# A two-layer perceiver block on one core: attention split by halves of the heads, a running maximum of the context, and new queues

## The chip, the cores and the metric

One core of one Trainium2 chip runs the whole program. The metric is device microseconds (us) from the first to the last instruction of one execution, with what lies around them; the median of three executions of the kernel before is 525.72 us (524.66 to 527.62). "Record" below means one instruction as the profile lists it.

## The reference, cut to what matters

The input has 8 batches of 64 tokens of width 128, and a context of 1601 rows for each batch. The kernel holds the 512 tokens as T = 4 tiles of 128 tokens (two batches each).

1. A stack of 4 layers. Each layer has causal self-attention with 16 heads of 8 elements, cross-attention to the first 32 rows of the context, and a gated feed-forward part of width 512. Before each of the three stands an RMS norm.
2. A message-passing block and a small feed-forward block.
3. Cross-attention to the whole context, with 2 heads of 64 elements.
4. One more self-attention layer with 16 heads (it runs through the same pieces as layer index 4).
5. A mixture of 8 experts, two of them chosen for each token.

```python
qkv = h @ Wqkv[l].T + bqkv[l]
q, k, v = jnp.split(qkv, 3, axis=-1)
q = apply_rope(split_heads(q, H), cos, sin)      # x * cos + rot(x) * sin
k = apply_rope(split_heads(k, H), cos, sin)
o = merge_heads(sdpa(q, k, v, causal_bias)) @ Wo[l].T + bo[l]
```

## The kernel before, in words

The work is cut into **pieces**. A piece is a short function of one engine for one layer or batch `i` and one tile or group `g`. `PIECES` lists them by engine with their counts: (4, 4) for the layers, (5, 4) for the parts that the last self-attention shares, (8, 4) for the context (8 batches, in 4 groups of 4, 4, 4 and 1 chunks of 128 rows). `PLACES` gives each piece its place in the queue of its engine. The engine works through its queue in that order and nothing else: a piece that waits holds back all that stands behind it. `BANKS` and `PLACED` say which of the 8 PSUM banks a piece of TensorE writes, and which piece frees it. Dependencies between engines are semaphore waits (`after`). The tables were made outside of the kernel; there is no planner in the code.

The pieces that matter here, for one tile of one layer, in the order of the data:

- `project` (PE, L804 to L809): four products, for Q, rotated Q, K and rotated K. `values` (L811): the V product.
- `rope` (DVE, L1321): multiplies all 512 columns by the cosines and sines. `rope_sum` (POOL, L1605) adds the two halves of Q and of K, `rope_bias` (POOL, L1610) adds the projection's bias after the rotation, and `k_groups` (POOL, L1615) spreads K over four head positions (128x512).
- `bias` (POOL, L1583 to L1594), once a layer: works the bias through the rotation, four operations.
- `causal`, `scores` (PE, L823, L831), `max` (DVE, L1331) and `shift` (DVE, L1334) over 1024 columns, `exp` (ACT, L1167), `turn` (PE, eight transposes, L839), `turned` (ACT, L1170), `weigh` (PE, L849; it needs `vblk`, DVE, L1326).
- Then `recip`, `o`, `turn_o`, `oT`, `out`, `y1` (DVE, L1353) end the self-attention. The cross-attention (L863 to L903, `y2`) and the gated part (L908 to L920, `y3`) follow.

The first pieces of TensorE's queue are `mem_vp.3` and `mem_vp.1` (L794), products for the cross-attention that need `wm`; the first `turn1` (L803) stands behind them.

For a batch `i` of the context: `c_moments` (DVE, L1452), `c_power` and half of the normalizing (POOL), `c_spread` (ACT, the other half), `c_turn`, `c_keys`, `c_scores` (PE), `c_squares` (ACT), `c_sums` (DVE), `c_rnorm` (POOL, L1674 and L1675), `c_scaled` (DVE, L1463). When all four groups are scaled, `top` (DVE) takes the maximum over the 13 chunks in one reduction (L1469) and over the tile's own scores (L1471). `top_turn`, `top_row`, `top_diag`, `top_spread` make of it one value for a column, `shifted` (DVE, L1483) subtracts it, `weights` (ACT, L1262) takes the exponentials, and `sum_ctx` (PE, L1063) sums.

The context of batch `b` is loaded by the SP queue (L1707) into one of two buffers. From the third batch on it waits until batch `b - 2` has been normalized (POOL) and spread (ACT). The experts' weights are loaded by the same queue before batch 4.

Of the kernel before, what the change touches and what calls it, by code (L numbers as in the profile page):

```python
# [14 lines left out]
P = 128  # L15
# [49 lines left out]
        "turn1": LAYERED5, "project": LAYERED5, "values": LAYERED5, "causal": LAYERED5, "scores": LAYERED5, "turn": LAYERED5,  # L65
        "weigh": LAYERED5, "turn_o": LAYERED5, "out": LAYERED5, "turn2": LAYERED, "qc": LAYERED, "cmask": LAYERED,
# [11 lines left out]
        "square1": LAYERED, "norm1": LAYERED, "hT1": LAYERED5, "exp": LAYERED5, "turned": LAYERED5, "oT": LAYERED5,  # L78
# [9 lines left out]
        "rope": LAYERED5, "vblk": LAYERED5, "max": LAYERED5, "shift": LAYERED5, "recip": LAYERED5, "o": LAYERED5, "y1": LAYERED5,  # L88
# [5 lines left out]
        "qk1_taken": TILED, "l_scaled": TILED, "c_moments": GROUPED, "c_sums": GROUPED, "c_scaled": GROUPED, "top": BATCHED,  # L94
# [6 lines left out]
        "mem_copy": (1, 1), "bias": (LAYERS + 1, 1), "x_zero": (2, 1),  # L101
        "pow1": LAYERED, "rope_sum": LAYERED5, "rope_bias": LAYERED5, "k_groups": LAYERED5, "base": LAYERED, "kc": LAYERED,
# [21 lines left out]
    "x_scaled": "qk1_taken l_scaled c_scaled top top_row top_diag shifted",  # L124
# [11 lines left out]
    "turn1": (1, "hT1"), "project": (1, "rope"), "values": (1, "vblk"), "causal": (4, "shift"), "turn": (2, "turned"),  # L136
    "weigh": (1, "o"), "turn_o": (1, "oT"), "out": (1, "y1"), "turn2": (1, "hT2"), "qc": (1, "qcT"), "cmask": (2, "cshift"),
# [15 lines left out]
HELD = {"scores": "causal", "cscores": "cmask", "up": "gate"}  # L153
# [3 lines left out]
    "mem_kp": (31, 59),  # L157
    "mem_vp": (23, 1, 4, 0, 46, 56, 49, 39),
    "turn1": (3, 2, 10, 9, 93, 85, 105, 111, 170, 161, 194, 209, 251, 238, 293, 277, 533, 515, 595, 620),
    "project": (7, 5, 16, 12, 95, 87, 107, 115, 173, 164, 197, 211, 254, 241, 295, 280, 536, 516, 597, 625),  # L160
    "values": (6, 11, 30, 17, 98, 88, 113, 120, 174, 169, 200, 214, 266, 243, 298, 282, 537, 517, 598, 626),
    "causal": (14, 8, 24, 19, 101, 91, 112, 124, 176, 167, 206, 216, 257, 247, 304, 284, 565, 523, 604, 628),
    "scores": (15, 13, 26, 20, 102, 96, 117, 125, 177, 175, 208, 221, 262, 250, 307, 292, 570, 526, 606, 631),
    "turn": (21, 18, 35, 29, 109, 103, 127, 132, 185, 180, 218, 226, 269, 259, 315, 301, 579, 535, 613, 635),
    "weigh": (28, 22, 40, 34, 114, 106, 130, 137, 187, 184, 222, 229, 272, 264, 319, 306, 587, 554, 617, 637),
    "turn_o": (32, 25, 45, 38, 118, 108, 135, 141, 190, 189, 225, 235, 275, 270, 324, 308, 599, 559, 621, 639),
    "out": (36, 27, 48, 44, 121, 110, 139, 144, 193, 191, 231, 237, 278, 273, 326, 312, 602, 561, 624, 641),
    "turn2": (43, 33, 55, 54, 126, 116, 145, 151, 198, 196, 236, 242, 286, 281, 329, 318),
# [1895 lines left out]
```

How the kernel before makes its waits and increments, by code:

```python
        def step(eng, name, instruction):  # L667
            instruction.then_inc(s[name], 1)
            steps[name] += 1
            eng.wait_ge(s[name], steps[name])
# [1 line left out]
        def after(eng, od, p, i, g=0):  # L673
            if i >= 0 and g >= 0:
                eng.wait_ge(s[SIGNAL.get(p, p)], od.count[p, i, g])
# [1 line left out]
        def after_all(eng, od, p, i):  # L678
            if i >= 0:
                eng.wait_ge(s[SIGNAL.get(p, p)], od.last(p, i))
# [18 lines left out]
        def take(pe, od, p, i, g):  # L699
            for users in od.bank[p, i, g][1]:
                for f, j, k in users:
                    pe.wait_ge(s[SIGNAL.get(f, f)], od.count[f, j, k])
            return held(od, p, i, g)
# [39 lines left out]
        def open_pool(pool):  # L744
            pool.wait_ge(s["par_set"], 1)
            pool.wait_ge(s["y_moments"], 1)
            nc.gpsimd.tensor_tensor(lg[:], mv[:, :, 1], par[:, 0:1].to_broadcast([P, T]), ALU.add).then_inc(s["y_power0"], 1)
            pool.wait_ge(s["y_power0"], 1)
            nc.gpsimd.tensor_tensor(rstd[:], lg[:], par[:, 1:2].to_broadcast([P, T]), ALU.pow).then_inc(s["y_power"], 1)
# [1 line left out]
        def open_dve(dve):  # L751
# [4 lines left out]
            nc.vector.memset(vblk[:], 0.0).then_inc(s["vector_step"], 1)  # L756
            steps["vector_step"] += 1
            dve.wait_ge(s["x_loaded"], 16)
            for t in range(T):
                last = nc.vector.bn_stats(st[:, t, :], x[:, t, :])
            last.then_inc(s["y_stats"], 1)
            dve.wait_ge(s["y_stats"], 1)
            for t in range(T):
```

## Time and profile before

| what | us |
|---|---|
| three executions: median, range | 525.72, 524.66 to 527.62 |
| the execution that was profiled | 524.75 |
| its span, first to last instruction | 522.5 |
| PE, DVE, ACT, POOL busy | 460.1, 361.8, 251.1, 252.9 |
| granted TensorE clock, mean | 0.97 of full |

The profiled execution is 2.25 us longer than its span and 0.97 us shorter than the median. A busy PE is not PE at its peak: records of small products overlap and their ends are modelled. The profile's page gives the busy time by engine, the chain of work that ended last, and groups of instructions by line; the trace behind it can be read in stretches. Stages overlap in this kernel: the layers run from some 15 to 253 us, the messages from 213 to 317, the context from 262 to 450, the last self-attention from 375 to 483, and the experts from 451 to the end.

### The profile page before, as it was taken

To read this page: it belongs to the slowest core of one execution; us is meant where nothing else is said; L and a number is where in the kernel's file an instruction comes from. 1 tells how busy PE (TensorE), PEld (TensorE's weight loads), DVE (VectorE), ACT (ScalarE), POOL (GpSimd) and SP (SyncE) were. 2 spreads that over 40 slices of the span, in tenths; PEclk is the share of its full clock that TensorE was granted. 3 is DMA by queue.
4 is the path that set the end of the run, shared out by engine and by line. 5 is a ranking of instruction groups with operands and counts; after the bars stand their busy time and mean duration, and the time that the engine had idled before them with its cause. 6 is when DMAs were issued, how large, how long until landed. Compare 5 with 4: busy or idle time off the path is not lost.

```text
span 522.5 us, 13720 instructions
## 1 busy us (share of the span) xinstructions
PE 460.1 (88%) x5309; PEld 394.9 (76%) x5318; DVE 361.8 (69%) x944; ACT 251.1 (48%) x592; POOL 252.9 (48%) x370
## 2 busy tenths in 40 slices
PE   2899889897989888999999898986877997999997
PEld 0676776776767767889899887874767886889897
DVE  4868877566656656665687787867686888764644
ACT  2275746754655656545544554423435645413221
POOL 4756786353545334203539994607879852230000
PEclk9999999999989999999999999976897999999999
DMA  8801102000201000000420005500120000000000
GB/s 228 357 3 56 56 1 63 28 10 11 62 3 37 2 1 2 3 3 3 140 68 3 2 3 216 235 1 15 50 65 1 1 1 1 2 1 1 13 0 16
DMA packets 8984, 23.02 MB, mean 44 GB/s; under 512 B 1217, under 2 KB 4817, under 8 KB 8658
## 3 DMA queue, kind: packets, MB, share of 16 engines
q1 hardware_dynamic: 8914, 22.07, 12.3%
q8 instruction: 46, 0.75, 0.6%
q14 instruction: 24, 0.20, 0.1%
HBM read 21.81 MB, written 0.26 MB: 42 GB/s over the span
## 4 chain that ended last, share of the span: by engine, by line
PE 64%; DVE 15%; POOL 10%; ACT 4%; issue 4%; DMA 1%; SPq 0%; DVEq 0%; ACTq 0%; POOLq 0%
PE ps L1133 6%; PE ps L1124 5%; PE ps L839 4%; PE ps L1063 4%; PE ps L849 3%; PE ps L1036 3%; PE ps L977 3%; PE ps L941 3%; POOL rk L1675 3%; PE ps L1048 2%; PE ps L808 2%; PE ps L908 2%; PE ps L1030 2%; PE ps L920 2%; POOL rsx L1658 2%
## 5 line engine op out<-in xcount | busy, mean ns | idle before, releaser
L1620 POOL TENSOR_TENSOR rstd<-ss,par 128x1 f32<-128x1 f32 x52 | 28.9, 559 | 55.9 <-ACT sq L1153 55.8
L1675 POOL TENSOR_TENSOR rk<-rk,par 128x8 f32<-128x8 f32 (+1 forms) x32 | 45.8, 1431 | 2.7
L1167 ACT ACTIVATE own<-own 128x1024 f32<-128x1024 f32 (+1 forms) x36 | 31.1, 864 | 20.5 <-DVE own L1334 13.3
L1633 POOL TENSOR_TENSOR rstd<-mv,par 128x1 f32<-128x1 f32 x24 | 5.0, 206 | 62.6 <-DVE mv L1388 62.2
L1063 PE MATMUL ps<-xh,own 128*128 128x130 f32 x208 | 29.1, 299 | 2.0 <-ACT own L1262 2.0
L1048 PE MATMUL ps<-own,xnT 128*128 128x128 f32 x208 | 29.2, 282 | 1.8 <-issue 0.6
L1133 PE MATMUL ps<-we,own 128*128 128x128 f32 x256 | 30.4, 276 | 0.0
L1133 PEld LDWEIGHTS ps<-we,own 128*128 128x128 f32 x256 | 29.7, 192 | 0.6 <-DVE x L1512 0.3
L1124 PE MATMUL ps<-hT,we 128*128 128x256 f32 x128 | 30.0, 384 | 0.0
L1063 PEld LDWEIGHTS ps<-xh,own 128*128 128x128 f32 x208 | 27.5, 212 | 3.0 <-issue 1.7
L1036 PE MATMUL ps<-xw,xnT 128*128 128x128 f32 x208 | 28.5, 285 | 1.2 <-ACT xnT L1252 1.2
L1048 PEld LDWEIGHTS ps<-own,xnT 128*128 128x128 f32 x208 | 28.5, 197 | 1.0
L1036 PEld LDWEIGHTS ps<-xw,xnT 128*128 128x128 f32 x208 | 26.1, 199 | 2.5 <-ACT xnT L1252 2.2
L1258 ACT ACTIVATE ksq<-ps 128x512 f32<-128x512 f32 (+1 forms) x32 | 16.4, 516 | 23.5 <-PE ps L1036 16.9
L1156 ACT ACTIVATE h<-y,rstd 128x128 f32<-128x128 f32 x48 | 19.0, 399 | 17.9 <-POOL rstd L1620 17.1
L1605 POOL TENSOR_TENSOR qk<-own 128x256 f32<-128x256 f32 x20 | 14.5, 727 | 26.5 <-DVE own L1321 26.5
L1331 DVE TENSOR_REDUCE mx<-ps 128x16 f32<-128x1024 f32 x20 | 24.4, 1220 | 4.3 <-PE ps L831 3.9
L1170 ACT COPY own<-ps 128x1024 f32<-128x1024 f32 x20 | 20.2, 1011 | 13.9 <-PE ps L839 13.9
L1124 PEld LDWEIGHTS ps<-hT,we 128*128 128x128 f32 x128 | 23.5, 190 | 3.5 <-issue 0.4
L849 PEld LDWEIGHTS ps<-vblk,own 128*64 128x64 f32 x640 | 20.5, 138 | 6.7 <-DVE own L1463 2.3
L839 PE MATMUL ps<-cf,own 128*128 128x128 f32 x160 | 23.0, 291 | 2.4 <-ACT own L1167 2.3
L1293 ACT ACTIVATE own<-ps,we 128x256 f32<-128x256 f32 x32 | 13.4, 471 | 24.4 <-PE ps L1124 17.3
(241 smaller groups left out, 1306.8 us busy)
## 6 DMA issues: line engine op xcount, KB each, us to landing
cx<-ctx_in SPq DMA_DIRECT2D x8, 768.0 KB
we<-we_in SPq DMA_DIRECT2D x8, 514.0 KB, 6.8
wc<-wc_in SPq DMA_DIRECT2D x4, 768.5 KB, 6.0
wa<-wa_in SPq DMA_DIRECT2D x5, 387.0 KB, 3.6
uvT<-uvT_in SPq DMA_DIRECT2D x1, 1024.0 KB, 10.5
uv<-uv_in SPq DMA_DIRECT2D x1, 1024.0 KB, 11.1
wb<-wb_in SPq DMA_DIRECT2D x4, 128.5 KB, 4.4
wm<-wm_in SPq DMA_DIRECT2D x1, 512.0 KB, 6.7
```

The source lines that it names most:

```text
L839: last = nc.tensor.transpose(bank[:, P * j:P * j + P], pr[:, g, P * j:P * j + P], ident)
L849: last = nc.tensor.matmul(bank[L * b:L * b + L, 18 * j:18 * j + 18], pts[:, g, P * j + L * b:P * j + L * b + L], vblk[:, g, b, j, :, :], s ...
L1036: last = nc.tensor.matmul(bank[:, P * j:P * j + P], xnT[n % 3][:, P * j:P * j + P], xw[:, X_K:X_K + P], start=True, stop=True)
L1048: last = nc.tensor.matmul(bank[:, P * j:P * j + P], xnT[n % 3][:, P * j:P * j + P], columns(qp[t][:, k, :, :]), start=False, stop=True, sk ...
L1063: last = nc.tensor.matmul(bank[:, 0:D + 2], sT[i][:, c, :], xh[i % 3][:, c, :], start=(c == 0), stop=(c == CT - 1))
L1124: last = nc.tensor.matmul(bank[:, 2 * P * c:2 * P * c + 2 * P], we[:, i, W_1 + P * c:W_1 + P * c + P], columns(hT[:, 2 * g:2 * g + 2, :]), ...
L1133: last = nc.tensor.matmul(bank[:, P * k:P * k + P], hid[g][i % 2][:, c, P * k:P * k + P], we[:, i, W_2 + P * c:W_2 + P * c + P], start=(c ...
L1167: done(nc.scalar.activation(pr[:, g, 0:k], sd[:, g, 0:k], ACT.Exp), p)
L1170: done(nc.scalar.copy(pts[:, g, :], held(od, "turn", i, g)), p)
L1331: done(nc.vector.tensor_reduce(mx[:, g, :].rearrange("p (r i) -> p r i", i=4), quad(od, i, g), AX, ALU.max), p)
L1620: done(nc.gpsimd.tensor_tensor(rstd[:, t:t + 1], ss[:, t:t + 1], par[:, 1:2], ALU.pow), p)
L1675: done(nc.gpsimd.tensor_tensor(rk[:, n, 0:2 * w], rk[:, n, 0:2 * w], par[:, 1:2].to_broadcast([P, 2 * w]), ALU.pow), p)
```

## The change: what it does, and the diff

- `project` makes K and rotated K alone; a new `project_q` makes Q and rotated Q, in a bank of its own.
- `rope` becomes `rope_k` and `rope_q`, two operations of 128 columns each, (product + bias) x cosine or sine. The bias is a column of the layer's weights, so `bias` and `rope_bias` are gone from POOL. The first `rope_k` of a layer waits for the load of `wa`.
- `rope_sum` becomes `k_sum` and `q_sum`. `k_groups` becomes `k_first` (two head positions, POOL) and `k_later` (the other two, ACT). `vblk` moves from DVE to ACT.
- `max`, `shift`, `exp`, `turn`, `turned` and `weigh` are split by halves of the heads (`max0`, `max1`, ...).
- `top` of the context becomes a running maximum: `c_top` after each group keeps a maximum of 256 columns in `mxr`, and a short `top` joins it.
- All queues and bank placements are new. TensorE begins with `turn1`, `values` and `project_q`; the `mem_vp` products follow.

```diff
-HELD = {"scores": "causal", "cscores": "cmask", "up": "gate"}
+HELD = {"scores": "causal", "weigh1": "weigh0", "cscores": "cmask", "up": "gate"}
...
             elif p == "project":
...
-                for k, w in enumerate((A_Q, A_QR, A_K, A_KR)):
+                for k, w in ((0, A_K), (1, A_KR)):
...
+            elif p == "project_q":
...
+                for k, w in ((0, A_Q), (1, A_QR)):
...
             elif p == "scores":
                 bank = held(od, p, i, g)
-                after(pe, od, "k_groups", i, g)
+                after(pe, od, "k_first", i, g)
+                after(pe, od, "k_later", i, g)
+                after(pe, od, "q_sum", i, g)
...
+            elif p in ("turn0", "turn_1"):
+                bank, k = take(pe, od, p, i, g), int(p[-1])
+                after(pe, od, "exp%d" % k, i, g)
+                for j in range(4):
+                    last = nc.tensor.transpose(bank[:, P * j:P * j + P], pr[:, g, 512 * k + P * j:512 * k + P * j + P], ident)
...
+            elif p == "k_later":
+                after(act, od, "k_sum", i, g)
...
+                for k in (2, 3):
+                    last = nc.scalar.activation(kblk[g][:, :, k, :], qk[:, g, 1, :].rearrange("p (b q) -> p b q", q=L), ACT.Copy, scale=hm4[:, k:k + 1])
...
+            elif p == "vblk":
+                after(act, od, "values", i, g)
...
-                done(nc.vector.tensor_tensor(columns(rope[g]), held(od, "project", i, g), columns(trig[:]), ALU.mult), p)
...
+            elif p in ("rope_k", "rope_q"):
+                if p == "rope_k" and leads(od, p, i, g):
+                    dve.wait_ge(s["wa_loaded%d" % (i % 2)], 32 * (i // 2 + 1))
...
+                    last = nc.vector.scalar_tensor_tensor(
+                        rope[g][:, n, :], held(od, "project" if p == "rope_k" else "project_q", i, g)[:, P * k:P * k + P],
+                        wa[i % 2][:, A_BQ + n:A_BQ + n + 1], trig[:, n, :], ALU.add, ALU.mult)
...
+            elif p == "c_top":
+                after(dve, od, "c_scaled", i, g)
+                if g == 0:
+                    after(dve, od, "top", i - 2)
+                    done(nc.vector.tensor_tensor(mxr[k][:], sT[i][:, 0:2, :], sT[i][:, 2:4, :], ALU.max), p)
+                elif g < 3:
+                    after(dve, od, "c_top", i, g - 1)
+                    step(dve, "vector_step", nc.vector.tensor_tensor(mxr[k][:], mxr[k][:], sT[i][:, 4 * g:4 * g + 2, :], ALU.max))
+                    done(nc.vector.tensor_tensor(mxr[k][:], mxr[k][:], sT[i][:, 4 * g + 2:4 * g + 4, :], ALU.max), p)
+                else:
+                    after(dve, od, "l_scaled", t)
+                    done(nc.vector.tensor_tensor(sm[k][:], sT[i][:, CT - 1, :], sl[t][:, k, :], ALU.max), p)
             elif p == "top":
                 after(dve, od, "top_turn", i - 2)
-                after_all(dve, od, "c_scaled", i)
-                step(dve, "vector_step", nc.vector.tensor_reduce(mxp[k][:], sT[i][:, 0:CT, :].rearrange("p c q -> p q c"), AX, ALU.max))
-                after(dve, od, "l_scaled", t)
-                done(nc.vector.tensor_tensor(mxp[k][:], mxp[k][:], sl[t][:, k, :], ALU.max), p)
+                after(dve, od, "c_top", i, 2)
+                step(dve, "vector_step", nc.vector.tensor_tensor(mxp[k][:], mxr[k][:, 0, :], mxr[k][:, 1, :], ALU.max))
+                after(dve, od, "c_top", i, 3)
+                done(nc.vector.tensor_tensor(mxp[k][:], mxp[k][:], sm[k][:], ALU.max), p)
...
+            elif p in ("k_sum", "q_sum"):
+                k = "qk".index(p[0])
+                after(pool, od, "rope_" + p[0], i, g)
+                done(nc.gpsimd.tensor_tensor(qk[:, g, k, :], rope[g][:, 2 * k, :], rope[g][:, 2 * k + 1, :], ALU.add), p)
+            elif p == "k_first":
+                after(pool, od, "k_sum", i, g)
...
+                done(nc.gpsimd.tensor_tensor(kblk[g][:, :, 0:2, :], qk[:, g, 1, :].rearrange("p (b q) -> p b q", q=L).unsqueeze(2).to_broadcast([P, 2, 2, L]),
```

Some stretches of the new queues, as `PLACES` orders them (layer or batch, then tile or group):

```
PE, start:    turn1.0.1 values.0.1 project_q.0.1 turn1.0.0 project.0.1 mem_vp.1 mem_vp.2 project.0.0 mem_vp.3 mem_vp.0 mem_vp.4 causal.0.1 scores.0.1
PE, 4 to 3:   sum_ctx.7.3 turn0.4.1 o_turn.2 u_turn.7 turn_1.4.1 heads.7 o_project.2 weigh0.4.1 weigh1.4.1 o_turn.3 turn_o.4.1 o_project.3
              turn1.4.2 out.4.1 values.4.2 project.4.2 project_q.4.2 turn1.4.3 causal.4.2 values.4.3 project_q.4.3 project.4.3 e_turn.1 scores.4.2 e_up.0.0
PE, before:   sum_ctx.7.3 scores.4.2 u_turn.7 e_turn.0 heads.7 e_logits.0 e_up.1.0
DVE, loads:   ... c_sums.3.1 c_moments.4.0 to c_moments.4.3, c_moments.5.0 totals.1 c_moments.5.1 ...
DVE, loads:   ... c_sums.4.3 c_moments.6.0 to c_moments.6.3 recip.4.0 shifted.3.2 ...
```

## Rows read from the trace of the kernel before

**Rows 1.** Stretches: length, busy PE, PEld, DVE, ACT, POOL, granted clock, DMA, GB/s.

```profile
26.00:208.00 182.00, 162.61 (x1984) 129.25 (x1984) 121.42 (x279) 108.51 (x284) 95.62 (x140) 0.99 0.08 24
...
260.00:442.00 182.00, 156.70 (x1528) 141.15 (x1535) 144.58 (x413) 85.92 (x181) 119.63 (x160) 0.92 0.13 49
...
82.50:131.80 49.30, 43.12 (x566) 33.95 (x564) 30.99 (x63) 28.97 (x77) 22.89 (x34) 1.00 0.06 18
```

**Rows 2.** A stretch of 13 us in the context, same columns.

```profile
351.00:364.00 13.00, 8.06 (x45) 6.10 (x44) 8.98 (x51) 4.61 (x12) 7.64 (x10) 0.63 0.00 1
```

**Rows 3.** The start of PE, in order of time: start, length, engine, line, operation.

```profile
10.34 3.75 PE L794 MATMUL ps<-wm,mem 128*128 128x512 f32 x4 [10.34 <-DMA wm<-wm_in]
...
15.28 1.05 PE L808 MATMUL ps<-hT,wa 128*128 128x128 f32 x8
```

**Rows 4.** Groups by line and form: busy us, mean ns, idle before and releasers.

```profile
L1321 DVE TENSOR_TENSOR own<-ps,trig 128x512 f32<-128x512 f32 x20 | 13.7, 687 | 4.7 <-PE ps L808 4.7
...
L1610 POOL TENSOR_TENSOR qk<-qk,qkb 128x256 f32<-128x256 f32 x20 | 14.6, 728 | 1.8
...
L1615 POOL TENSOR_TENSOR own<-qk,cf 128x512 f32<-128x512 f32 x20 | 20.9, 1044 | 1.4
...
L1592 POOL TENSOR_TENSOR qkb<-qkt 128x128 f32<-128x128 f32 x5 | 2.3, 455 | 0.4
...
L1365 DVE TENSOR_TENSOR y<-ps,y 128x128 f32<-128x128 f32 x32 | 9.2, 288 | 15.9 <-PE ps L903 8.2 <-PE ps L920 7.6
...
L1163 ACT ACTIVATE hT<-ps,wa 128x128 f32<-128x128 f32 x20 | 7.0, 362 | 9.2 <-PE ps L803 9.1
```

**Rows 5.** The same view, softmax: rows of whole width, then of half width.

```profile
L1334 DVE TENSOR_TENSOR own<-ps,mx 128x1024 f32<-128x1024 f32 x20 | 24.5, 1224 | 0.6
...
L1167 ACT ACTIVATE own<-own 128x1024 f32<-128x1024 f32 x20 | 21.1, 1054 | 13.4 <-DVE own L1334 13.3
...
L1359 DVE TENSOR_TENSOR own<-ps,mx 128x512 f32<-128x512 f32 x16 | 11.0, 688 | 0.4
...
L1167 ACT ACTIVATE own<-own 128x512 f32<-128x512 f32 x16 | 10.0, 627 | 7.0 <-DVE own L1359 6.9
...
L1173 ACT COPY own<-ps 128x512 f32<-128x512 f32 x16 | 9.3, 583 | 3.1 <-PE ps L886 2.8
```

**Rows 6.** Waits of PE from 26 to 208 us: total, times, longest.

```profile
PE ps L831 <- POOL own L1615: 3.8, 4, 1.4
```

**Rows 7.** The same view as rows 4: the context's maximum over all chunks.

```profile
L1469 DVE TENSOR_REDUCE mxp<-own 128x128 f32<-128x1664 f32 x8 | 24.4, 3050 | 0.5
```

**Rows 8.** The chain that ended last, from 262 us on: start, us, what.

```profile
326.41 3.06 DVE mxp L1469
...
346.80 5.87 PE ps L1063 x26
...
382.28 3.10 DVE mxp L1469
...
436.24 2.88 PE ps L1063 x24
```

**Rows 9.** In order of time: the last operation of `top` twice, POOL beside the first.

```profile
310.50 0.74 DVE L1471 TENSOR_TENSOR mxp<-mxp,own 128x128 f32<-128x128 f32 x1
...
310.05 1.04 POOL L1671 TENSOR_TENSOR xh<-xh,rsx 128x512 f32<-128x512 f32 x1
...
341.82 0.29 DVE L1471 TENSOR_TENSOR mxp<-mxp,own 128x128 f32<-128x128 f32 x1
```

**Rows 10.** In order of time: last sum of the context, first expert product.

```profile
447.55 0.38 PE L1065 MATMUL ps<-ones,own 64*128 64x1 f32 x2
...
450.94 1.76 PE L1124 MATMUL ps<-hT,we 128*128 128x256 f32 x7
```

**Rows 11.** In order of time: the load of batch 6 and the statistics that read it.

```profile
363.72 0.34 SPq L1707 DMA_DIRECT2D cx<-ctx_in  x1
...
373.93 0.86 DVE L1452 BATCH_NORM_STATS2 stx<-cx 128x6 f32<-128x128 f32 x4
```

More of the change, by code:

```diff
@@ L100 @@
     "POOL": {
-        "mem_copy": (1, 1), "bias": (LAYERS + 1, 1), "x_zero": (2, 1),
-        "pow1": LAYERED, "rope_sum": LAYERED5, "rope_bias": LAYERED5, "k_groups": LAYERED5, "base": LAYERED, "kc": LAYERED,
+        "mem_copy": (1, 1), "x_zero": (2, 1),
+        "pow1": LAYERED, "k_sum": LAYERED5, "k_first": LAYERED5, "q_sum": LAYERED5, "base": LAYERED, "kc": LAYERED,
         "pow2": LAYERED, "pow3": LAYERED, "pow_f": TILED,
@@ L135 @@
     "mem_kp": (1, "mem_k"), "mem_vp": (1, "mem_v"),
-    "turn1": (1, "hT1"), "project": (1, "rope"), "values": (1, "vblk"), "causal": (4, "shift"), "turn": (2, "turned"),
-    "weigh": (1, "o"), "turn_o": (1, "oT"), "out": (1, "y1"), "turn2": (1, "hT2"), "qc": (1, "qcT"), "cmask": (2, "cshift"),
+    "turn1": (1, "hT1"), "project": (1, "rope_k"), "project_q": (1, "rope_q"), "values": (1, "vblk"), "causal": (4, "shift0 shift1"), "turn0": (1, "turned0"), "turn_1": (1, "turned1"),
+    "weigh0": (1, "o"), "turn_o": (1, "oT"), "out": (1, "y1"), "turn2": (1, "hT2"), "qc": (1, "qcT"), "cmask": (2, "cshift"),
     "cturn": (1, "cturned"), "cweigh": (1, "co"), "cturn_o": (1, "coT"), "cout": (1, "y2"), "turn3": (1, "hT3"),
@@ L403 @@
-    "top_turn": "04775334",
-    "top_spread": "47371264",
-    "sum_ctx": "47317073",
-    "u_turn": "01315073",
-    "heads": "01315273",
-    "o_turn": "6623",
-    "o_project": "6623",
-    "e_turn": "2156",
-    "e_logits": "26",
-    "e_cho": "70",
-    "e_b2": "60",
-    "e_up": "4606426220460440",
-    "e_down": "3121406223637230",
+    "mem_kp": "32",
+    "mem_vp": "34212012",
+    "turn1": "20301221532720005231",
+    "project": "53203200711310212233",
+    "project_q": "01320422603204340500",
@@ new lines @@
+    "values": "10121131532725205511",
+    "causal": "44444440004444440444",
+    "turn0": "02221141040323510254",
+    "turn_1": "10242076772252137000",
+    "weigh0": "31023101060333516004",
+    "turn_o": "33023131020613517060",
+    "out": "33323131010653511065",
+    "turn2": "3103621021321404",
+    "qc": "3103621021341214",
+    "cmask": "6042446400624224",
+    "cturn": "3345372413100122",
+    "cweigh": "3135072413130024",
+    "cturn_o": "3133022413130022",
+    "cout": "2403021443200034",
@@ new lines @@
+    "bwv_p": "6",
+    "c_turn": "23575164070215611476736203101217",
+    "c_keys": "25575101027212301475724631701415",
+    "c_scores": "20207654350323743450352627360451",
+    "top_turn": "71017321",
+    "top_spread": "34614721",
+    "sum_ctx": "50563303",
+    "u_turn": "11211343",
+    "heads": "11742323",
+    "o_turn": "0711",
+    "o_project": "0721",
+    "e_turn": "6160",
+    "e_logits": "06",
+    "e_cho": "01",
+    "e_b2": "55",
+    "e_up": "0220602404262242",
+    "e_down": "4516751407765747",
@@ L606, in program @@
         rqk = sb("rqk", [P, T, 4], F32, later)
+        mxr = [sb(f"mxr{i}", [P, 2, P], F32, later) for i in range(2)]
+        sm = [sb(f"sm{i}", [P, P], F32, later) for i in range(2)]
         mx1 = [sb(f"mx1{i}", [P, 1], F32, later) for i in range(2)]
```

538 lines of the change are left out of this document (253 added, 285 removed), and 38 rows, old and new, of the table PLACES.

## Prediction

> **What bounds the kernel now.** I read the stretches first, then the chain of waits, then single groups. In the layers, 26 to 208 us, PE is busy 162.6 of 182 us, DVE 121 and ACT 109 [rows 1]: PE leads, with 19.4 us idle. One layer takes 49.3 us, from one `y1` of tile 1 to the next, and PE is busy 43.1 of them [rows 1]. The reader is to see that the layers can give back about 6 us each in idle time and no more, whatever is done to the other engines. In the context, 260 to 442 us, PE is busy 156.7, DVE 144.6 and POOL 119.6 of 182 us at a mean granted clock of 0.92 [rows 1]: no engine is full there, so the order of hand-overs sets the time. The chain holds the 3 us reduction of `top` three times [rows 8]. Around it the granted clock falls: 0.63 from 351 to 364 us, with PE busy 8.06 of 13 [rows 2]. A sum over the context that takes 2.88 us for 24 records at 436 us took 5.87 us for 26 at 347 us [rows 8], which is the price of the lower of the clock's two levels, 1.2 in place of 2.4 GHz.
>
> **The change, part by part.** The sum is made against the profiled execution, 524.75 us, which is 1.0 us below the median of the runs shown. A measurement of this kernel can tell about 0.5% (2.6 us) from no change.
>
> *K ahead of Q, the bias in the rotation.* The path from the projection to `scores` was `rope` 0.69 + `rope_sum` (same form as `rope_bias`, 0.73) + `rope_bias` 0.73 + `k_groups` 1.04 = 3.2 us [rows 4]. The new path is two 128-column DVE operations with PSUM input, 0.29 each (the nearest row, L1365), `k_sum` 0.46 (the 128-column sum), and `k_first`, which writes 256 columns: 0.73 by the 256-column row. Together 1.8 us [rows 4]. `k_later` on ACT, two operations of at most 0.36, stands beside `k_first`. K is also ready two products earlier. Q's two operations (0.58) and sum (0.46) come in where K's end, so I take 1.5 us per tile and layer off this path, not the whole.
>
> *Softmax by halves.* Before: maximum and subtraction 1.22 each (the row shows the subtraction; both read the same 1024 PSUM columns) and exponential 1.05, so 3.5 us [rows 5]. After: four half-width DVE operations at 0.69 and one exponential at 0.63 behind the last, 3.4 us; the first half's transposes, copy (0.58) and weighing run meanwhile, so half of each, about 0.5 + 0.5 + 0.6 us, leaves the path [rows 5]. I take 1.7 us. Where the new queue puts `turn_1` ahead of `turn0` less is won.
>
> *What the layers give back.* 3.2 us from a chain of a tile that shares PE with three others. Nothing lies directly on PE's waits but 3.8 us for K's groups [rows 6]; the rest must come out of the other 15.6 us of idle time. Bounds: 0 (other tiles already fill the gap) and 4 x 3.2 = 13 us (every layer shortens by it). I take 8, nearer to the middle because the idle time is 19.4 us in all and waits that the change doesn't touch stay.
>
> *Added work.* DVE per tile and layer: four operations of 0.29 in place of 0.69, two of 0.69 in place of 1.22 twice over, less `vblk`, whose place ACT takes: under 0.8 us more, in a stage where DVE has a third free. ACT gets `k_later`, `vblk` and the halves' second starts, about 0.7 + 0.7 + 0.4 us; 16 times that is 29 us on top of 109 of 182 [rows 1, 4]. The cover is ACT's idle 73 us. If a copy is in front of `k_later`, `scores` and its four PSUM banks wait for it, one copy 0.58 at a time [rows 5]. I take +1, bounds 0 to +4. POOL loses work everywhere. The new wait of `rope_k` for `wa` costs nothing: the load is issued two layers ahead.
>
> *The start.* PE began at 10.34 with two products on `wm`, 3.75 us, and the first projection came at 15.28 [rows 3]. Now `turn1` stands first. POOL's first power moves ahead of `mem_copy` too. The first tile can gain up to 4.7 us, but five `mem_vp` products now stand before its scores, the same work for PE later. Bounds 0 and -4.7; I take -1.5.
>
> *The running maximum.* After the last scaling of a batch, 3.05 + 0.29 us become one 128-column operation of `c_top` and two of `top`, 0.9 us: 2.4 us less latency [rows 7, 9]. It was on the chain in three of eight batches [rows 8], so -7; bounds 0 and 8 x 2.4 = -19. DVE's total hardly changes. No row shows a maximum of 256 columns with both inputs in SBUF. 0.29 (128 columns) and 0.69 (512) bound it [rows 4, 9]; in the middle, 0.42, five of them and three short ones make 3.0 us for a batch against 3.3.
>
> *The port that POOL and DVE share.* The same `top` operation took 0.74 us in place of 0.29 where POOL normalized beside it [rows 9]. The new maxima are 64 operations of that kind, the old reduction had none of it. POOL's normalizing covers some 34 us of the stage (32 operations of 1.04), a fifth, so some 12 operations may be hit by 0.45 us each, 5 us on DVE, a third on the path: +1.5, bounds 0 and +8. The Trainium skill has the rule for it (SBUF — State Buffer, Who interferes with whom): a DVE instruction with two SBUF inputs and a GpSimd instruction that reads SBUF exclude each other for a whole instruction. By that rule every POOL operation counts, not the normalizing alone. This speaks against the change; it is a rival below.
>
> *The clock.* If PE no longer waits for `top`, the low clock may stay away; the one sum of rows 8 alone is 2.7 us of it. Bounds: -7 (all of it) and +7 (as much anew elsewhere). I take -3.
>
> *Ahead of the experts.* Before, the first expert product came 3.4 us after the last context sum, 447.55 to 450.94 [rows 10]. In the new queue two tiles' projections and the chain last sum, `heads`, `o_turn`, `o_project`, `a_norm`, `turn1.4.3`, `project.4.3` stand in front of it, about 11 us with 8 us of PE work. PE idles some 3.5 us where it idled 1. I take +3, bounds +1 and +10 (the work at half the clock). What follows is PE's own work at full rate, the same in sum.
>
> Sum: 524.75 - 8 + 1 - 1.5 - 7 + 1.5 - 3 + 3 = 510.75, rounded to **511 us**.
>
> **The rivals.**
> (A) The gains add up: layers -13, maximum -12, clock -7, the rest as above less its costs: 497 us. For it: both chains are cut in all tiles. Against: 43.1 of 49.3 us are PE's already.
> (B) The path was hidden. Other tiles fill PE and the next hand-over is late in its place; only the start and some waits fall away: -8 becomes -1, -7 becomes -1, 524 us. For it: PE waits for K only four times [rows 6].
> (C) Slower: DVE's queue stands behind a context load. The new queue puts the statistics of batches 4 and 5 in one block ahead of the totals and maxima that PE's sums need, and those of batch 6 ahead of `recip.4.0`. In the trace the statistics of batch 6 began 10.2 us after the load was issued, with other work between [rows 11]; the load itself waits for POOL's normalizing (4 x 1.04 us). Four such blocks, each some 5 us late, are +20 and give 531; from 14 us in all it outweighs the gain. For it: the DVE work between `rope_k.4.0` and that block is 9 us, the chain to the load's end about 8, which is a thin margin. Against: for batches 4 and 5 I count 28 us of DVE work ahead of the block.
> (D) The port decides. If most of the 64 maxima are hit, 64 x 0.45 = 29 us on DVE, and 538 us. By the rule of the Trainium skill above this could happen. Against: DVE has 37 us idle in the stage and POOL's operations on a few columns were many of its busy us.
>
> **How the numbers follow.** Forecast 0.50, (A) 0.14, (B) 0.14, (C) 0.17, (D) 0.05. Faster by over 0.5%: 0.50 + 0.14 + a fifth of (B) = 0.67. Within: the rest of (B), 0.11. Slower: 0.22. The range takes in the forecast with its bounds, nearly all of (A), (B), and the lower half of (C): 498 to 530.
>
> **What would show it.** The layer period of tile 1 should fall from 49.3 to some 47 us, and PE's wait for K's groups should go. `top` should leave the chain, and the sums over the context should take about 3 us each. Ahead of the first expert product there should be a stretch with PE half idle. The forecast is wrong if the layers keep their period with PE idle as before (B), if DVE's idle time ends on context statistics that wait for a DMA (C), or if the maxima's mean is well over 0.45 us (D).

## The result and the profile after

The changed kernel takes 505.34 us (median of 4 runs, 502.99 to 505.84), against 526.67 us for the kernel before beside it (median of 4). The ratio is 0.9589, 95% interval 0.9543 to 0.9635: 21.6 us less by the ratio. A ratio leaves out executions more than 1.5% above the fastest of their kernel, so it need not be the quotient of the two medians beside it. Forecast were 511 us, 498 to 530. The profiled execution took 505.84 us, with a span of 504.0 us, 18.5 us below the span of before.

First the head of the page of the kernel after: busy time of each engine, 40 slices of the span, the chain by engine.

```profile
PE 459.4 (91%) x5307; PEld 395.4 (78%) x5318; DVE 355.1 (70%) x1052; ACT 275.7 (55%) x712; POOL 226.2 (45%) x350
...
PE   1998899999999999989979999987889998999996
...
PEclk9999989989999999999989999989998999999999
...
PE 76%; DVE 9%; ACT 5%; issue 4%; POOL 3%; DMA 2%; SPq 1%; ACTq 0%; DVEq 0%; POOLq 0%
```

PE is busy 459.4 us, as before (460.1). So its idle time fell from 62.4 to 44.6 us, 17.8 of the span's 18.5 us: nearly the whole gain is idle time of PE.

Now the stretches of after, in the columns of [rows 1]: the start, the layers as in [rows 1], from the last `y3` to the last context sum, the gap ahead of the experts, the experts.

```profile
0.00:26.00 26.00, 15.58 (x110) 9.83 (x111) 16.68 (x50) 10.35 (x31) 10.35 (x24) 1.00 0.83 294
26.00:208.00 182.00, 169.72 (x2058) 136.60 (x2059) 122.74 (x330) 128.87 (x380) 76.39 (x128) 0.98 0.08 24
...
249.70:419.50 169.80, 156.04 (x1707) 141.75 (x1716) 149.35 (x481) 91.59 (x200) 128.37 (x172) 0.96 0.18 61
419.50:432.90 13.40, 11.82 (x118) 8.85 (x118) 7.76 (x28) 5.49 (x17) 3.79 (x9) 0.87 0.01 2
432.90:504.00 71.10, 66.12 (x518) 60.26 (x512) 37.28 (x123) 20.41 (x50) 2.90 (x7) 0.99 0.02 6
```

The same stretches of before:

```profile
0.00:26.00 26.00, 14.13 (x115) 9.26 (x116) 17.20 (x42) 6.30 (x19) 15.51 (x29) 1.00 0.85 294
...
253.00:447.60 194.60, 168.12 (x1838) 151.60 (x1838) 153.99 (x435) 92.96 (x194) 128.12 (x174) 0.93 0.15 54
447.60:450.90 3.30, 2.89 (x35) 1.99 (x34) 2.72 (x4) 0.79 (x3) 0.24 (x1) 1.00 0.02 5
450.90:522.50 71.60, 67.81 (x530) 61.82 (x529) 38.90 (x128) 20.11 (x46) 4.67 (x9) 1.00 0.02 6
```

The last `y3` comes at 249.7 us in place of 253.0, only 3.3 us earlier, though PE idles 7.1 us less from 26 to 208 us (12.3 against 19.4 [rows 1]): part of that stretch's work is work that was due later. From there to the last sum it takes 169.8 us in place of 194.6. Of these 24.8 us, 12.7 are idle time of PE (13.8 in place of 26.5). The other 12.1 are busy time: the stretch holds 131 fewer PE records, and its clock is 0.96 in place of 0.93. The gap to the first expert product is 13.4 us in place of 3.3, with products of the last self-attention in it. The experts take the same.

The prediction named a layer's period, from one `y1` of tile 1 to the next, as its first sign: 49.3 us should become some 47. In the same layer it became 51.1 (82.17 to 133.28 us), with PE busy 48.2 us of it in place of 43.1. The layer behind it took 43.4 us in place of 51.8. Over the three periods from the first layer to the last the sum fell from 150.8 to 145.1 us. One layer's period is no measure here, since the new order moves work between layers.

Two more readings. From 400 us on, in order of time, the last sums over the context and the first expert product:

```profile
405.05 4.87 PE L1077 MATMUL ps<-xh,own 128*128 128x130 f32 x42
...
416.33 3.15 PE L1077 MATMUL ps<-xh,own 128*128 128x130 f32 x26 [0.27 <-DVE o L1547]
...
432.88 1.34 PE L1138 MATMUL ps<-hT,we 128*128 128x256 f32 x5
```

And the groups by line of DVE, 255 to 460 us, with the new maxima (two of `c_top`, the last step of `top`, the first of `c_top`); columns as in [rows 4]:

```profile
L1507 DVE TENSOR_TENSOR mxr<-mxr,own 128x256 f32<-128x256 f32 x16 | 9.0, 560 | 0.5
...
L1506 DVE TENSOR_TENSOR mxr<-mxr,own 128x256 f32<-128x256 f32 x16 | 7.5, 471 | 0.2
...
L1503 DVE TENSOR_TENSOR mxr<-own 128x256 f32<-128x256 f32 x8 | 3.3, 416 | 0.0
L1516 DVE TENSOR_TENSOR mxp<-mxp,sm 128x128 f32<-128x128 f32 x8 | 3.1, 391 | 0.5 <-DVE mxp L1514 0.3
```

A sum of 26 records takes 3.15 us, at a granted clock of 1.00, where one took 5.87 us [rows 8], at 0.52. An undisturbed 256-column maximum takes 0.42 us, as estimated. Here are two of these maxima, each with the POOL operation beside it (start, length, engine, line):

```profile
308.40 0.42 DVE L1507 TENSOR_TENSOR mxr<-mxr,own 128x256 f32<-128x256 f32 x1
307.97 1.92 POOL L1715 TENSOR_TENSOR rk<-rk,par 128x8 f32<-128x8 f32 x1
...
315.99 1.15 DVE L1507 TENSOR_TENSOR mxr<-mxr,own 128x256 f32<-128x256 f32 x1
315.63 1.22 POOL L1709 TENSOR_TENSOR xh<-cx,mvx 128x512 f32<-128x512 f32 x1
```

The first lies wholly within a POOL operation on 8 columns and takes no longer for it. Of all 64 maxima in this trace, 54 overlap a POOL operation. Ten of them overlap one of the normalizing, 128x512, and six of these ten took longer: five 1.09 to 1.15 us, one 0.55. The other 44, beside POOL operations on 1 to 13 columns and once on 128, took their usual time. POOL's times in the profile are rough, but the seven other traces with such maxima show the same; the only two exceptions stand beside POOL sums of 128 and 256 columns.

### The profile page after: what moved, and what is told of

Same layout as the page of the kernel before. It is cut to its first block, busy times and chain, and to the rows that moved or that the text cites. A ratio compares the mean times of both kernels' runs of the same rounds, so it can differ in the third digit from the quotient of the medians.

```text
span 504.0 us, 14043 instructions
## 1 busy us (share of the span) xinstructions
PE 459.4 (91%) x5307; PEld 395.4 (78%) x5318; DVE 355.1 (70%) x1052; ACT 275.7 (55%) x712; POOL 226.2 (45%) x350
## 3 DMA queue, kind: packets, MB, share of 16 engines
q1 hardware_dynamic: 8914, 22.07, 12.7%
## 4 chain that ended last, share of the span: by engine, by line
PE 76%; DVE 9%; ACT 5%; issue 4%; POOL 3%; DMA 2%; SPq 1%; ACTq 0%; DVEq 0%; POOLq 0%
PE ps L1147 6%; PE ps L1138 6%; PE ps L1062 5%; PE ps L1050 5%; PE ps L863 4%; PE ps L1077 4%; PE ps L853 3%; PE ps L922 3%; PE ps L991 3%; PE ps L927 3%; PE ps L934 3%; PE ps L955 3%; PE ps L845 2%; PE ps L1044 2%; PE ps L814 2%
## 5 line engine op out<-in xcount | busy, mean ns | idle before, releaser
L1195 ACT ACTIVATE own<-own 128x512 f32<-128x512 f32 x56 | 34.5, 628 | 14.1 <-DVE own L1366 9.7
L1650 POOL TENSOR_TENSOR qk<-own 128x128 f32<-128x128 f32 x40 | 18.1, 455 | 34.8 <-DVE own L1354 34.5
L1361 DVE TENSOR_REDUCE mx<-ps 128x8 f32<-128x512 f32 x40 | 26.0, 684 | 10.2 <-PE ps L845 9.8
L1354 DVE SCALAR_TENSOR_TENSOR own<-ps,wa,trig 128x128 f32<-128x128 f32 x80 | 23.3, 341 | 12.6 <-PE ps L820 8.0
L1077 PE MATMUL ps<-xh,own 128*128 128x130 f32 x208 | 26.1, 277 | 1.3 <-ACT xnT L1281 0.7
L1281 ACT ACTIVATE xnT<-ps,xw 128x512 f32<-128x512 f32 (+1 forms) x32 | 21.7, 697 | 10.1 <-PE ps L1044 4.7
L1077 PEld LDWEIGHTS ps<-xh,own 128*128 128x128 f32 x208 | 24.4, 190 | 3.0 <-ACT xnT L1281 1.0
L809 PE MATMUL ps<-cf,h 128*128 128x128 f32 x52 | 15.7, 308 | 12.0 <-ACT h L1170 11.2
L1366 DVE TENSOR_TENSOR own<-ps,mx 128x512 f32<-128x512 f32 x40 | 26.3, 678 | 0.0
L1199 ACT COPY own<-ps 128x512 f32<-128x512 f32 x40 | 22.6, 588 | 5.7 <-PE ps L853 5.4
```

What stands on the lines that cost most here:

```text
L1077: last = nc.tensor.matmul(bank[:, 0:D + 2], sT[i][:, c, :], xh[i % 3][:, c, :], start=(c == 0), stop=(c == CT - 1))
L1195: done(nc.scalar.activation(pr[:, g, a:a + 512], sd[:, g, a:a + 512], ACT.Exp), p)
L1199: done(nc.scalar.copy(pts[:, g, 512 * k:512 * k + 512], held(od, ("turn0", "turn_1")[k], i, g)), p)
L1354: last = nc.vector.scalar_tensor_tensor(rope[g][:, n, :], held(od, "project" if p == "rope_k" else "project_q", i, g)[:, P * k:P * k + P], ...
L1361: done(nc.vector.tensor_reduce(mx[:, g, 8 * k:8 * k + 8].rearrange("p (r i) -> p r i", i=4), quad(od, i, g)[:, 2 * k:2 * k + 2, :, :], AX, ...
L1366: done(nc.vector.tensor_tensor(sd[:, g, 512 * k:512 * k + 512].rearrange("p (r i k) -> p r i k", i=4, k=L), quad(od, i, g)[:, 2 * k:2 * k ...
```

## The experiments

Twelve kernels were timed beside the kernel before, in 5 to 12 executions each. "Against after" is the difference of the ratios times 526.67 us. An interval of a ratio is 0.0025 to 0.0055 either way, and after's own is 0.0046, so the last column is known to about 3 us.

| kernel | median, us | ratio to before (95%) | against after |
|---|---|---|---|
| new order, old pieces (order_alone) | 545.46 | 1.0335 (1.0301 to 1.0369) | +39 |
| new pieces, old order (pieces_alone) | 536.73 | 1.0165 (1.0122 to 1.0208) | +30 |
| after without running maximum (new_no_max) | 519.34 | 0.9854 (0.9829 to 0.9878) | +14.0 |
| after with whole-width softmax (new_whole) | 512.57 | 0.9701 (0.9676 to 0.9726) | +5.9 |
| after with the old rotation (new_old_rot) | 524.76 | 0.9937 (0.9902 to 0.9973) | +18.3 |
| before with running maximum (old_max) | 534.31 | 1.0137 (1.0092 to 1.0183) | |
| before with softmax halves (old_halves) | 527.16 | 1.0006 (0.9974 to 1.0039) | |
| before with the new rotation (old_rot) | 537.13 | 1.0178 (1.0122 to 1.0233) | |
| new pieces at merged places (merged_places) | 522.13 | 0.9860 (0.9816 to 0.9904) | +14.3 |
| after with before's start (new_old_start) | 504.16 | 0.9541 (0.9500 to 0.9583) | -2.5 |
| after, K's groups all on POOL (new_k_pool) | 506.80 | 0.9582 (0.9541 to 0.9622) | -0.4 |
| after, sums of K and Q made twice (new_sums_twice) | 511.02 | 0.9670 (0.9623 to 0.9717) | +4.3 |

### The order alone, and the pieces alone

```diff
 # order_alone: after's queues, each pair of parts merged at the place of its later one
+PLACES["project"] = [max(pair) for pair in zip(PLACES["project"], PLACES["project_q"])]
+PLACES["rope"] = [max(pair) for pair in zip(PLACES["rope_k"], PLACES["rope_q"])]
+for name, n in (("rope_sum", 0.2), ("rope_bias", 0.4), ("k_groups", 0.6)):
+    PLACES[name] = [max(three) + n for three in zip(PLACES["k_sum"], PLACES["k_first"], PLACES["q_sum"])]
...
-            elif p == "c_top":
+                step(dve, "vector_step", nc.vector.tensor_reduce(mxp[k][:], sT[i][:, 0:CT, :].rearrange("p c q -> p q c"), AX, ALU.max))
```

> The new order with the old pieces: the four projections in one piece, the rotation, its sum, the bias and the groups of K as before, maximum, subtraction and exponential over the whole width, one reduction for top. A merged piece stands where the later of its two parts stood; V's blocks stay with ACT, and the transposes stay in two pieces of one bank. Before takes 526.7 us, after 505.3. Theory 1 (shorter chains give the time, the order only has to let them): 524 to 530, since only the start gains. Theory 2 (the order gives it): 505 to 512. Theory 3 (order and pieces pay only together): above 532.

```diff
 # pieces_alone: before's queues, the second part right behind the first
+PLACES["max1"] = [p + 0.1 for p in PLACES["max0"]]
+PLACES["rope_q"] = [p + 0.1 for p in PLACES["rope_k"]]
+        scaled = PLACES["c_scaled"][4 * b + c] + 0.1
...
```

> The new pieces in the old order: rotation with bias, K's two sums ahead of Q's, softmax by halves, running maximum, each part put where the old piece stood, the second half right behind the first. Not in it: K's products ahead of Q's, the last two groups of K on ACT, V's blocks on ACT. Theory 1 (shorter chains): before's 526.7 less 8 for the layers and 7 for top and 3 for the clock, plus 2.5 of costs, about 511. Theory 2 (the order gives it): 524 to 528. Theory 3 (only together): 516 to 524.

Measured: the order alone is 3.35% slower than before, the pieces alone 1.65% slower, both together 4.11% faster. My theory (each shorter chain gives its gain, whatever the order) gave 524 to 530 and 511 and missed both; the rival that the order gives it all missed too. The first of the two stood in the range of theory 3, and the second was worse than it said. The pieces alone are also not quite the same pieces: the last groups of K and V's blocks stay where they were, as the expectation says. The order alone also spoils the layers: its last `y3` stands at 272.6 us, after's at 249.7. How far that is the merging is the question of merged_places below.

### Each piece taken out of after

```diff
 # new_no_max
-            elif p == "c_top":
...
+                after_all(dve, od, "c_scaled", i)
+                step(dve, "vector_step", nc.vector.tensor_reduce(mxp[k][:], sT[i][:, 0:CT, :].rearrange("p c q -> p q c"), AX, ALU.max))
```

> After, with top as one reduction over the nine tiles again and no running maximum; the rest and the order stay. My term for it was 7 us with bounds 0 and 19, with another 3 for the clock. Theory 1: 512 to 515 us, with the 3 us reduction back on the chain. Rival (the new order hides top as well as it hides the rest): 505 to 507, and the reductions off the chain.

+14.0 us, more than Theory 1 had. The chain from 250 us on has the reduction in all eight batches; before it had three [rows 8]. Start, us, what:

```profile
296.76 3.04 DVE mxp L1502
311.77 2.91 DVE mxp L1502
...
340.21 2.90 DVE mxp L1502
356.19 2.94 DVE mxp L1502
...
380.18 3.00 DVE mxp L1502
...
396.86 3.01 DVE mxp L1502
409.70 3.07 DVE mxp L1502
419.74 3.02 DVE mxp L1502
```

The layers are untouched (last `y3` 250.7 us), and from there to the last sum it takes 181.0 us in place of 169.5. That is 11.5 of the 14 us. DVE's own work in the two is alike: the old form is 24.1 + 4.0 = 28.1 us, the new one 27.5. So it is latency and not DVE's work. Eight batches by the 2.4 us estimated in the prediction would be 19 us; 11.5 are seen in the stretch.

```diff
 # new_whole: parts merged at the later place; max, shift and exp one operation each
-    ... "causal": (4, "shift0 shift1"), ...
+    ... "causal": (4, "shift"), ...
...
 # new_old_rot: likewise the products, and the path of the kernel before
+            elif p == "rope_bias":
+            elif p == "k_groups":
```

> After, with softmax of the self-attention over the whole width: one maximum, one subtraction and one exponential, at the place of the later half, and the transposes, copies and weighing of the two halves side by side at the later place. Theory 1: the halves gave 1.7 of the 3.2 us per tile and layer, so some 4 of the 8 us of the layers come back: 508 to 511 us. Rival (hidden by other tiles): 505 to 506.5. Theory 3 (an order laid out for halves loses more without them than they gave): above 513.

> After, with the old path from the projection to the scores: four products in one piece, one rotation, its sum, the bias and K's groups on POOL, each at the place of the latest of the pieces it stands for. V's blocks stay on ACT. Theory 1: the path is 1.5 us longer for each tile and layer, so some 4 of the layers' 8 us come back: 508 to 511 us, and PE waits for K's groups again. Rival (hidden): 505 to 506.5. Theory 3: above 513.

+5.9 and +18.3 us. By its median the first lies between Theory 1 and theory 3, the second lies well within theory 3. Both also merge places, which the next experiment takes apart. PE's waits from 26 to 208 us in new_old_rot (total, times, longest):

```profile
PE ps L848 <- POOL own L1662: 9.2, 8, 2.1
```

Before this wait was 3.8 us [rows 6], in after 0.8 and 0.2 us. By PE's waits the old path, merged places included, costs the new order more than it cost the old one.

### The same queue with either kind of pieces

```diff
 # merged_places against order_alone: same places and banks, new pieces
+PLACES["k_sum"] = [max(three) + 0.2 for three in zip(PLACES["k_sum"], PLACES["k_first"], PLACES["q_sum"])]
...
```

> The control for the order alone (545 us): the same merged places and the same banks, each pair of parts at the place of its later one, but with the new pieces: bias in the rotation, K's rotation and sum ahead of Q's, the last two groups of K on ACT, softmax by halves right behind each other, the running maximum at its own places. The four products stay in one piece. Theory 1 (it is the shorter chains that the new order needs): what the three single removals lost comes back, 545 less 14, 7 and some of 19, so 508 to 518. Rival (a merged or shifted place is what costs, whatever the pieces are): above 530. Between 518 and 530 both have a part.

-4.75% of before against order_alone, 25 us, so within one queue the pieces are worth more than the whole gain; but the merged places cost 14 us against after. Both have a part, as the middle case of the expectation has it, and by stage they can be told apart. When did the last `y3` and the last sum come (first and last start, us, after the durations)? First order_alone:

```profile
L1387 DVE TENSOR_TENSOR y<-ps,y x32: 279/292/294, 49.9 to 272.6; 128x128 f32<-128x128 f32 x32
...
L1084 PE MATMUL ps<-xh,own x208: 272/275/378, 330.5 to 456.2; 128*128 128x130 f32 x104
```

Then merged_places:

```profile
L1402 DVE TENSOR_TENSOR y<-ps,y x32: 277/291/294, 54.1 to 269.7; 128x128 f32<-128x128 f32 x32
...
L1081 PE MATMUL ps<-xh,own x208: 272/275/378, 326.7 to 440.5; 128*128 128x130 f32 x104
```

In the context the pieces (the running maximum) give 183.6 - 170.8 = 12.8 us, beside the 11.5 of new_no_max. In the layers they give 2.9 us, and the merging takes 20.0 (269.7 against 249.7). By its profile 2.9 is rather too small and 20.0 too large: the profiled execution of merged_places, 526.28 us, is its longest of six, 4 us above the median, and not counted in its ratio. Its clock from 26 to 208 us is 0.95 in place of 0.98, some 5 us of the 20 by an estimate from these two figures. One layer, the second, is nearly free of merging: merged_places needs 50.6 us for it from last `y3` to last `y3`, after 50.3. There new_old_rot needs 56.7, order_alone 56.2, new_whole 51.4 and before 58.5. So the new rotation path is worth 6 us in such a layer and the halves 1. PE's wait for K's groups in that layer, 89 to 141 us, first order_alone, which needs 56.2:

```profile
PE ps L852 <- POOL own L1650: 3.7, 4, 1.7
```

then after (the wait for a sum; there is none for the groups):

```profile
PE ps L845 <- POOL qk L1650: 0.2, 1, 0.2
```

### The path to the scores, without merging

```diff
 # new_sums_twice
+                step(pool, "pool_step", nc.gpsimd.tensor_tensor(qk[:, g, k, :], rope[g][:, 2 * k, :], rope[g][:, 2 * k + 1, :], ALU.add))
                 done(nc.gpsimd.tensor_tensor(qk[:, g, k, :], rope[g][:, 2 * k, :], rope[g][:, 2 * k + 1, :], ALU.add), p)
 # new_k_pool
-                after(pe, od, "k_later", i, g)
-            elif p == "k_later":
```

> After, with K's sum and Q's sum on POOL each made twice, one after the other with the same result; nothing is merged and no place changes. It puts 0.46 us into the path to the scores (0.9 where Q's sum stands ahead), for each tile and layer, without the merged places that the earlier undoings brought with them. In the one layer where merging moves nothing apart, the old path, about 1.5 us longer, cost 6 us for four tiles. Theory 1 (PE waits for this path almost one to one in the new order): 4 tiles by 5 layers by 0.5 to 0.9 us, a third to a half of it seen, plus 4 to 8, so 509 to 513 us. Rival (only the merged places cost, other tiles hide the path): 505 to 507. If POOL's queue carries it on to the context too: above 515.

> After, with all four groups of K written by POOL in one operation at k_first's place, and ACT's k_later gone. The path to the scores is some 0.3 us longer for each tile and layer, Q's sum comes 0.3 us later where it stands behind, and ACT has two starts less, 0.7 us. Theory 1 (PE's waits for K carry it): 506 to 508 us. Rival (ACT, at over two thirds busy in the layers, was the later one of the two): 502 to 505.

Made twice, the sums cost 4.3 us by the ratio, at the lower end of what Theory 1 expected. The two intervals just touch. The second layer takes 52.8 us in place of 50.3, and the last `y3` comes 8.7 us later (258.4). PE's waits in it, 89 to 141 us:

```profile
PE ps L845 <- POOL qk L1651: 2.4, 2, 1.2
PE ps L845 <- POOL own L1656: 1.2, 2, 0.9
```

At 0.45 us for each extra sum, twenty tile-layers have 9.1 us of it on K's path alone: about a half is seen in the time, though nearly all of it at the end of the layers. That shows the layers of the new order to wait for POOL's sums, at untouched places; K's sum and Q's were not tried apart. K's groups all on POOL make no difference that can be measured: the median of 506.80 us stands in Theory 1's range, but before ran longer beside it too, and by the ratio it is -0.4 us, or 504.7, in the rival's range. Its last `y3` comes 5.3 us later than after's (255.0), 1.8 us are left of it at the first expert product (434.67), and nothing measurable at the end. So the time of the last `y3` is a weak measure of what the layers give to the whole. The two operations of `k_later` on ACT take 0.39 us each, and POOL's operation falls from 1.04 to 0.61 us by them.

### Each piece put into before

```diff
 # old_max
+        scaled = PLACES["c_scaled"][4 * b + c] + 0.1
+        mxr = [qkt, sb("mxr", [P, 2, P], F32, later)]
+        sm = mxp
 # old_halves
+PLACES["max1"] = [p + 0.1 for p in PLACES["max0"]]
 # old_rot
+                        wa[i % 2][:, A_BQ + n:A_BQ + n + 1], trig[:, n, :], ALU.add, ALU.mult)
...
```

> Before, with the running maximum alone, each part right behind its scaling. Theory 1: 526.7 less 7 to 10, 517 to 520, with PE's low clock before the sums of the context gone. Rival (the next hand-over in its place is as late): 525 to 527. If DVE pays for the many small maxima: above 528.

> Before, with the softmax of the self-attention by halves alone, the second half right behind the first. Theory 1: 4 us of the layers, 522 to 524. Rival (hidden by the other tiles): 526 to 528. Worse than that (above 529), if the halves' further starts on DVE and ACT hold up other tiles' work.

> Before, with the bias in the rotation alone: K's two rotations and its sum ahead of Q's, K's groups on POOL right behind K's sum. The four products stay one piece, and no work moves to ACT. Theory 1: the path to the scores is 1.1 us shorter, some 3 us of the layers, 522 to 525. Rival (hidden): 526 to 527.5.

The halves alone do nothing that can be measured (1.0006), as the rival said. The rotation alone costs 9.4 us, the running maximum alone 7.2: both outside what Theory 1 or the hiding rival allowed, and for the maximum the last line of the expectation holds. In old_rot DVE is busy 370.8 us in place of 361.8: four operations of 0.34 us stand where one of 0.69 stood, and here nothing was moved to ACT. So a rival to the order stands for the rotation: that DVE's 9 us of added work cost it, and not the place. No kernel with the old order and V's blocks on ACT was timed. Each part also had one place only in these kernels, right behind what it follows; other places in the old order were not tried.

For old_max the trace shows what happened at the first batch. DVE in order of time, first before: the reduction stands in one block, and DVE waits behind it anyway, for POOL:

```profile
290.54 3.02 DVE L1469 TENSOR_REDUCE mxp<-own 128x128 f32<-128x1664 f32 x1
...
298.14 0.89 DVE L1463 TENSOR_TENSOR own<-ps,rk 128x128 f32<-128x128 f32 x2 [1.82 <-POOL rk L1675]
```

Then old_max, four maxima ahead of a tile's statistics, POOL and PE behind them, and the same wait, longer:

```profile
287.06 0.69 DVE L1482 TENSOR_TENSOR qkt<-qkt,own 128x256 f32<-128x256 f32 x1
287.78 0.43 DVE L1483 TENSOR_TENSOR qkt<-qkt,own 128x256 f32<-128x256 f32 x1
288.31 0.43 DVE L1482 TENSOR_TENSOR qkt<-qkt,own 128x256 f32<-128x256 f32 x1
288.77 0.42 DVE L1483 TENSOR_TENSOR qkt<-qkt,own 128x256 f32<-128x256 f32 x1
289.12 0.28 DVE L1396 BATCH_NORM_STATS2 st<-h 128x6 f32<-128x128 f32 x1
289.70 0.19 POOL L1654 TENSOR_TENSOR rstd<-mv,par 128x1 f32<-128x1 f32 x1 [2.23 <-DVE mv L1397]
...
293.47 0.63 PE L1039 MATMUL ps<-cf,xh 128*128 128x128 f32 x4 [1.37 <-POOL xh L1692]
...
303.19 0.29 DVE L1472 TENSOR_TENSOR own<-ps,rk 128x128 f32<-128x128 f32 x1 [2.48 <-POOL rk L1696]
```

And PE of old_max, which waits and then runs slower. The 64 products at 307.76 took 1.99 us, at a granted clock of 0.50; the like ones at 303.58 took 1.16, at 1.00:

```profile
303.58 1.16 PE L966 MATMUL ps<-own 64*64 64x64 f32 x64 [1.97 <-issue]
...
307.76 1.99 PE L977 MATMUL ps<-qh,own 64*64 64x64 f32 x64
```

The old order had given the 3 us block a place where DVE had to wait for POOL's `rk`; cutting it there saved nothing. The maxima moved 2 us of DVE work ahead of the statistics that POOL waited 2.23 us for, and PE waited 1.37 us for POOL behind it. The kernel was 2.8 us late before any of this, where the two programs do the same (PE's transpose at 265.81 us, 263.02 before), 5.0 at the tile's statistics (289.12, 284.17 before), 7.9 at the first sum (312.6, 304.7 before). Read from the order of events, and not tested by itself, the maxima explain about 2 us directly, and the wait with the low clock behind it 3 more. The other batches were not followed in this way.

### The start

```diff
+PLACES["mem_vp"] = (9, -2, -1, 8, 10, 19, 20, 29)
```

> After, with two of the memory's products (those of layers 1 and 2) at the head of PE's queue again, ahead of the first transpose, as before had it; one of them gets another bank. My term for the start was 1.5 us with bounds 0 and 4.7. Theory 1: 506 to 508 us. Rival (the first scores come 0.7 us earlier and no more, the rest is absorbed by other idle time): 505 to 506. If the first tile carries it all: 509 to 510.

504.16 us, ratio 0.9541: no loss, less than any case of the expectation. PE begins with the two products as in [rows 3], and the first scores come at 20.15 us in place of 19.31:

```profile
10.13 3.78 PE L803 MATMUL ps<-wm,mem 128*128 128x512 f32 x4 [10.13 <-POOL mem L1629]
...
20.15 0.69 PE L848 MATMUL ps<-own,qk 32*64 32x256 f32 x16
```

The 0.8 us are gone by the first expert product, which comes at 432.2 us against 432.9. Whether this version is better than after is not settled: their intervals overlap.

## Why the prediction was right, and where it was not

**The total** came out 5.7 us under the forecast, inside the range, and for the reason given at the top: the gain is PE's idle time. The sum was better than its terms: the terms for the halves and the start were too large, the one for the maximum too small, and that they nearly cancel is luck. Two of the signs it named did not show: the layer period of tile 1 rose, and PE was not half idle ahead of the experts but busy 11.8 of 13.4 us.

**Layers, -8 + 1.** PE's idle time from 26 to 208 us fell by 7.1 us, but the last `y3` came only 3.3 us earlier. K's path (I took 1.5 us of the 3.2) is the part that counts: 6 us for the second layer, at merged places. The halves (1.7 of the 3.2) were oversized: 1.1 us in that layer, none in the old order. What they and the other splits give is mostly that each part can have a place of its own: merging them all, but for the maximum, costs 14 us. How much of it falls to the halves is open, since the 5.9 us of new_whole hold their merging too.

**Added work.** DVE from 26 to 208 us went from 121.4 to 122.7 us, though the rotation's operation takes 0.34 us, not 0.29. ACT took 20.4 us more, not 29. That its idle time covers this was not tested for V's blocks; with K's groups taken off ACT the time stayed the same.

**Start, -1.5.** The idle time of the first 26 us fell by 1.5 us, as forecast. By new_old_start (-2.5 us, with some 3 either way) a gain of 1.5 us in the whole is hardly possible. This term counted a local gain as one of the total.

**Running maximum -7 and clock -3.** Together -10; new_no_max measured 14.0. `top` was taken as critical in three of eight batches, since it was so in the old chain. In the new order without the running maximum it is on the chain in all eight. The term was mis-sized by 4 of 14 us. The clock of the stage rose from 0.93 to 0.96, and no sum of 26 records without a break took over 3.15 us. What the clock gave by itself was not tried.

**Port, +1.5.** The 48 maxima of the four rows above are 9.0 + 7.5 + 3.3 + 3.1 = 22.9 us; at 0.42 and, for the last row, 0.28 us they would be 19.0. So 3.9 us on DVE where I had 5; the share of it on the path was not measured. (D) is rejected: no group's mean is far above 0.45 us but one, 0.56. The premise of (D), that every POOL operation counts, did not hold: 6 of 54 overlapping maxima took longer, all beside the normalizing. The rule weighed for it (the Trainium skill, SBUF — State Buffer, Who interferes with whom) has a DVE instruction with two SBUF inputs contend with a GpSimd instruction that reads SBUF. The traces agree beside 128x512 operations and not beside those on few columns, where a 0.42 us maximum ran inside a 1.92 us POOL operation; the measurement decides.

**Ahead of the experts, +3.** The idle time there rose from 0.4 to 1.6 us, and at the granted clock of 0.87 some 13% of 13.4 us is lost, 1.7, by an estimate from that clock: together 2.9. That this meets the +3 is luck in part. I had 3.5 us idle where 1 was, so 2.5 more; 1.2 more were measured, and the clock was no part of the term.

**The rivals.** (A) had the maximum at 12, nearer to the 14 measured than my 7, but 13 for the layers. (B) holds for the halves in the old order, which gave nothing there; that the other two would cost, none of the rivals had. (C) did not occur: from 208 to 433 us DVE has one wait for a load, 0.8 us, and not for the context.

**The step that was missing** is the condition under all the terms. I priced each cut chain by its length and the old chain of waits, as if its gain stood by itself. By the runs nearly the same pieces (without what moved to ACT) cost 8.7 us in the old order, and they give 25 us in the new one (at merged places). The prediction was right because it was made for both together. The same pricing, used on the pieces alone, gave 511 us and the wrong sign: 536.7 were measured.

Open is how the cost of merging (14 us by the ratio) divides among the pairs, whether the rotation cost the old order its time by place or by DVE's added work, and why the order alone runs at a lower clock (0.956 over the span in place of 0.975, PE busy 10.3 us more than after): whether idle time or low clock came first was not tried.

## What to carry to other kernels

In a kernel whose queues are written out, a shorter chain is worth what the order makes of it: read whether the long operation stands where its engine would wait anyway, as `top` did behind POOL, and whether its pieces then go ahead of work that others wait for. Split an operation together with a new order, and test it both ways, with the old pieces in the new order and the new ones in the old. A gain of a microsecond at the start that no later wait inherits is not a gain, and a stage that ends earlier need not be one either: a last `y3` 5.3 us later cost nothing measurable here.

## What was not expected

The signs depended on the order, for the rotation with the rival named above. Taken out of the new one, the maximum, the halves and the rotation lose 14.0, 5.9 and 18.3 us, the last two with their merged places. Put into the old one, the maximum and the rotation lose 7.2 and 9.4 us, and the halves nothing measurable (0.3).

All four kernels with new parts in the old order also ran at a slightly lower clock. Over all their executions the median granted clock is 0.950 to 0.957, and 0.960 or 0.961 for the kernel before beside them (0.954 to 0.971). The profiled executions alone overstate it: before's, at 0.971, is as high as any of its own. The halves lost clock too (0.957) without losing time, and new_whole, 5.9 us slower than after, ran at the higher clock (0.987 against 0.976). So a mean clock by itself does not tell which of two orders is faster.
